# Products without a reader on TensorE in its waits, and GpSimd's last additions moved behind the logits

## The reference, cut to what matters

```python
x = x + 0.5 * quant_ffn(ln(x))          # int8 rounding of tokens and weight, 256 -> 256
x = x + linear_attention(ln(x))         # elu(q) + 1, elu(k) + 1, no softmax
x = x + 0.5 * quant_ffn(ln(x))
x = x + 0.5 * routed_mlp(ln(x))
x = x + softmax_attention(ln(x))
x = x + 0.5 * routed_mlp(ln(x))

def routed_mlp(x):                      # per batch
    logits = x @ Wr + br
    weights, idx = top_k(logits, 128)   # 128 of 1024 tokens, in order of their index
    tokens = sort(idx)
    out = gelu(x[tokens] @ W1 + b1) @ W2 + b2
    return x.at[tokens].add(softmax(weights) * out)
```

## Time and profile before

| | us |
|---|---|
| median of three runs | 3504.67 |
| lowest and highest | 3502.99, 3505.31 |
| the profiled execution, its own time | 3506.28 |
| its span, first to last instruction | 3504.5 |

### The profile page before, as it was taken

How to read it: one execution, slowest core, us unless ns; L and a number is a source line. 1 busy time by engine, 2 the same in 40 slices (tenths; PEclk the granted TensorE clock), 3 DMA queues, 4 the chain that set the end, 5 groups by cost and what they waited for, 6 DMA issues and landing times.

```text
span 3504.5 us, 52704 instructions
## 1 busy us (share of the span) xinstructions
PE 3339.6 (95%) x19398; PEld 2861.0 (82%) x19398; DVE 2666.2 (76%) x4957; ACT 2044.9 (58%) x3908; POOL 1057.1 (30%) x1274
## 2 busy tenths in 40 slices
PE   3898999989999999999999999999999999999995
PEld 2777878868888888888888888888888888888884
DVE  5788796767876787876788677886778767876776
ACT  3676767646556556556565556555555565556552
POOL 3786656632222112122121221212212131213112
PEclk8999999999999999999999999999999999999997
DMA  2221212110001000001000001000000010001000
GB/s 83 70 85 50 66 55 70 58 37 13 13 19 29 15 13 13 15 23 28 13 14 13 25 19 43 13 13 25 25 14 14 13 34 28 16 19 29 26 19 20
DMA packets 98525, 104.21 MB, mean 30 GB/s; under 512 B 10336, under 2 KB 88800, under 8 KB 98144
## 3 DMA queue, kind: packets, MB, share of 16 engines
q1 hardware_dynamic: 98272, 100.85, 9.7%
HBM read 87.18 MB, written 13.63 MB: 29 GB/s over the span
## 4 chain that ended last, share of the span: by engine, by line
PE 70%; DVE 6%; ACT 3%; DMA 0%; issue 0%; POOL 0%; DVEq 0%; SPq 0%; ACTq 0%; POOLq 0%
PE at_ps_job L1927 12%; PE at_ps_job L35 7%; PE at_ps_job L37 7%; PE at_ps_job L36 6%; PE at_ps_o L35 6%; PE at_ps_o L37 6%; PE at_ps_o L36 6%; PE at_ps_s L35 6%; PE at_ps_s L36 6%; PE at_ps_s L37 6%; DVE at_neg_max L1854 1%; ACT x_resident L1678 1%; DVE at_probT_lo L1721 1%; PE at_ps_job L646 1%; DVE at_oT_lo L1752 0%; DVE ch_r L97 0%
## 5 line engine op out<-in xcount | busy, mean ns | idle before, releaser
L1637 ACT ACTIVATE at_probT_hi<-at_ps_job 128x512 fp32r<-128x512 f32 x1024 | 611.4, 598 | 889.9 <-PE at_ps_job L1927 887.2
L1721 DVE TENSOR_TENSOR at_probT_lo<-at_ps_job,at_probT_hi 128x512 fp32r<-128x512 f32 x1024 | 702.8, 686 | 275.5 <-ACT at_probT_hi L1637 265.1
L1678 ACT ACTIVATE x_resident<-at_ps_s,at_neg_max 128x1024 f32<-128x1024 f32 x512 | 570.7, 1115 | 151.6 <-DVE at_neg_max L1854 146.5
L1854 DVE TENSOR_REDUCE at_neg_max<-at_ps_s 128x1 f32<-128x1024 f32 x512 | 622.2, 1215 | 5.3
L1927 PE MATMUL at_ps_job<-ident,x_resident 128*128 128x128 f32 x4096 | 613.7, 272 | 5.0 <-DVE at_probT_lo L1721 3.4
L1927 PEld LDWEIGHTS at_ps_job<-ident,x_resident 128*128 128x128 f32 x4096 | 495.9, 140 | 97.7 <-issue 7.3
L35 PE MATMUL at_ps_o<-at_probT_hi,at_v_lo 128*128 128x512 f32 x1024 | 446.3, 436 | 8.9 <-DVE at_oT_lo L1752 7.8
L1613 POOL TENSOR_TENSOR at_w_hi<-at_w_raw,ch_cols 128x256 fp32r<-128x256 f32 x192 | 117.6, 613 | 1107.1 <-PE at_ps_job L37 1086.3
L35 PE MATMUL at_ps_s<-at_k_hi,at_q_lo 128*128 128x512 f32 x1024 | 445.1, 435 | 0.0
L37 PE MATMUL at_ps_o<-at_probT_lo,at_v_hi 128*128 128x512 f32 x1024 | 404.6, 395 | 0.0
L36 PE MATMUL at_ps_s<-at_k_hi,at_q_hi 128*128 128x512 f32 x1024 | 402.0, 393 | 0.0
(11 more groups left out here) (347 smaller groups left out, 7480.8 us busy)
## 6 DMA issues: line engine op xcount, KB each, us to landing
at_w_raw<-attn_w SPq DMA_DIRECT2D x256, 128.0 KB, 2.3
at_w_raw<-mlp_w SPq DMA_DIRECT2D x112, 128.0 KB, 2.3
li_wo_hi<-li_wo_kept SPq DMA_DIRECT2D x24, 256.0 KB, 2.7
li_wo_lo<-li_wo_kept SPq DMA_DIRECT2D x24, 256.0 KB, 3.0
li_wq_hi<-li_wq_kept SPq DMA_DIRECT2D x48, 128.0 KB, 2.3
li_wq_lo<-li_wq_kept SPq DMA_DIRECT2D x48, 128.0 KB, 2.8
x_resident<-x SPq DMA_DIRECT2D x4, 1024.0 KB, 13.1
out<-x_resident SPq DMA_DIRECT2D x4, 1024.0 KB, 4.9
```

What stands on the lines that cost most here:

```text
L1637: nc.scalar.activation(ph[:, i // TC, 4 * half:4 * half + 4, (i % TC) * P:(i % TC + 1) * P], c.turned_bank(2 * TB * u + 2 * i + half), ACT ...
L1678: nc.scalar.activation(prob[:, slot % 2, :], ps_s[slot % 2][:], ACT.Exp, bias=nmax[:, slot:slot + 1], accum_out=rsum[:, u % 2, slot:slot + ...
L1721: nc.vector.tensor_tensor(pl[at], c.turned_bank(2 * TB * u + 2 * i + half), ph[at].bitcast(F32), ALU.subtract).then_inc(s_pl, 1)
L1854: nc.vector.tensor_reduce(nmax[:, slot:slot + 1], ps_s[slot % 2][:], AX.X, ALU.max, negate=True).then_inc(s_max, 1)
```

## The change

Six places change. A helper issues `count` products with the bfloat16 identity as the stationary operand, each with 512 bfloat16 columns; each starts and stops its own accumulation and no engine reads its result before the bank is written anew. It is called

- in the first layer, after the turns of the weight's scales, 34 times, into the last bank of `ps_y`;
- in the linear attention at the head of PE's stream, 22 times, into bank 7;
- in the last layer, into `ps_job[0]`, 20 times before `rows_out(1)` and behind the waits ahead of it, 24 times before `gather(0)`, 20 times before `gather(1)`.

And GpSimd waits for `f_l` to reach 2, which is when all eight tiles have their logits, before its eight additions in the last layer.

```diff
+def idle_products(nc, sh, bank, moving, count):
+    for _ in range(count):
+        nc.tensor.matmul(bank, sh.identb[:], moving, start=True, stop=True)
...
             last.then_inc(s_wt, 1)
+            idle_products(nc, sh, ps_y[-1][:].rearrange("p a d -> p (a d)"), wq[:].rearrange("p a d -> p (a d)"), 34)
             pe.wait_ge(s_v, 10)
...
+            idle_products(nc, sh, ps[:, 7, :], sh.wqT[:].rearrange("p k d -> p (k d)"), 22)
             pe.wait_ge(s_ones, 2 * TB)
             for t in range(BEGIN, plan.end):
...
             ln_rstd(nc, pool, sh, ln, 1, 4, 4)
+            pool.wait_ge(f_l, 2)
             for j in range(TB):
                 pool.wait_ge(f_half, j + 1)
...
             pe.wait_ge(c.took, max(by_act.values()))
+            idle_products(nc, sh, ps_job[0][:], sh.wqT[:].rearrange("p k d -> p (k d)"), 20)
             rows_out(1)
+            idle_products(nc, sh, ps_job[0][:], sh.wqT[:].rearrange("p k d -> p (k d)"), 24)
             gather(0)
+            idle_products(nc, sh, ps_job[0][:], sh.wqT[:].rearrange("p k d -> p (k d)"), 20)
             gather(1)
```

## The result

The changed kernel takes **3496.46 us** (median of 19 executions, 3495.21 to 3499.31); the kernel before takes 3504.97 us (19 executions, 3502.99 to 3506.37). The ratio is 0.9978, with an interval of 0.9971 to 0.9984: 8.5 us by the medians, 0.22 to 0.24% faster. That is past the 0.2% line of the prediction, but the interval (0.16 to 0.29%) reaches to both sides of it. The profiled execution after took 3497.92 us with a span of 3495.9, so the two spans differ by 8.6 us, like the medians.

A forecast was written before the change was run, and what follows sets the result against it. PE was taken to bound the long middle and VectorE to set the end. The terms -1.6 - 3.6 + 0.5 - 0.5 + 0.5 - 1.9 = -6.6 us, from the median 3504.67, gave 3498.1 us, range 3494.4 to 3502.2.

The forecast's parts named there:

- (1): First layer, 34 products after the weight's turns: costed at nothing, hidden by GpSimd's run of additions.
- (2): Start of the linear attention, 22 products: second low part sooner by 0.9 to 2.6 us, taken as -1.6.
- (3): Last layer, GpSimd's additions held behind the logits: VectorE's normalisations -1.5 and dot products -2.1, together -3.6 us.
- Rival C: Last layer: GpSimd's additions slow VectorE's comparisons, +3.5 on the forecast, 3501.6 us; chance 0.08.
- (4): Last layer, 20 products before the second row of logits: +0.5 us late (0 to 2.1), four turns faster, -0.5.
- (5): Last layer, 24 and 20 products around the first gather: +0.5 us late (0 to 1.6), second gather faster, -1.9.
- (6): Hidden layer's second half, at low clock before: whether shifted work meets that fall unreadable, taken as 0 (0 to -1.4).
- A: Whole kernel: the clock holds everywhere, no late filler, hidden layer 1.4 us shorter: -10.0, 3494.7 us; chance 0.20.
- B: Start: nothing gained, the clock falls in pauses or lower clock later eats the advance: -5.0, 3499.7 us; chance 0.22.
- D: Start and last layer: fillers outlast their gaps, all at the low clock: +7.9, 3512.6 us; chance 0.04.
- E: Whole kernel: fillers run, clock moves at other times, only GpSimd's wait counts: -3.6 + 1.0 late, 3502.1 us; chance 0.06.

The follow-up runs named there:

- experiment 5: The change without the 34 products of the first layer: 3499.18 us, ratio 0.9984 to the kernel before.
- experiment 8: The change with 7 more products behind the linear attention's first turns and 20 at the head of the attention's PE stream: 3498.14 us, ratio 0.9978.
- experiment 2: The change without GpSimd's wait, all products kept: 3499.89 us, ratio 0.9988 to the kernel before.
- experiment 4: The kernel before with the 34 and the 22 products at the start alone: 3503.61 us, ratio 1.0.
- experiment 6: The change without the 22 products of the linear attention: 3498.64 us, ratio 0.9983 to the kernel before.
- experiment 1: The kernel before with GpSimd's wait added and no products: 3502.01 us, ratio 0.9996.
- experiment 10: The change with GpSimd's additions held back further, behind the eighth comparison instruction: 3502.37 us, ratio 0.9993 to the kernel before.
- experiment 9: The change with products of 254 columns in six waits of PE for VectorE in the linear attention: 3493.90 us, ratio 0.9970 to the kernel before.
- experiment 12: Experiment 9 without the 34 products of the first layer, with a seventh place and more products: 3493.51 us, ratio 0.9968 to the kernel before.
- experiment 11: The change without the 20 products before the second row and the 24 before the first gather: 3500.29 us, ratio 0.9989 to the kernel before.
- experiment 3: The kernel before with only the last layer's 20, 24 and 20 products, without the wait: 3502.05 us, ratio 0.9991.
- experiment 7: The change with 40, 48 and 40 products in the last layer, twice as many: 3506.51 us, ratio 1.0005 to the kernel before.

## Why the prediction was right, and where it was not

The forecast was 3498.1 with a range of 3494.4 to 3502.2; 3496.46 lies in it. The direction had 0.42 for faster by over 0.2% and 0.54 for within it; it came out at 0.22 to 0.24%, so near the line that another set of runs could fall on the other side, and which side it fell on is luck. The mechanism is the forecast's, but three sizes were off, in both directions: the start won less, no filler of weight was late, and the hidden layer won 1.2 that was put at nothing. By the steps:

**(1) 34 products, 0: right** by the stages, and so was the cover: GpSimd's additions, which stand where they stood with them and without (experiment 5). The medians can't confirm it to better than some 3 us.

**(2) 22 products, -1.6: -1.1** at the second low part and -1.5 at the last statistics. The mechanism was the one foreseen, a fall of the clock in the middle of the products. But its size is not one number. Over the ten profiled executions that have the 22 (the 7 more of experiment 8 among them) the second low part stood between 49.57 and 51.98, and over before and the three without them between 51.70 and 52.18; the means, experiment 8 left out, are 50.9 and 52.0. The two values in which the clock held without the 7, 49.57 and 49.65, were those whose 22 products took longest (7.39 and 7.82 us, 6.3 to 7.2 in the others); in experiment 2 PE's first work behind them came late, at 43.87, and the clock was low from the second product on. That the lead is carried to the end was assumed. It is shown as far as the first query: from the second low part to there all these executions took 44.7 to 45.1 us. Behind it the stretch to the attention scatters between 621.2 and 625.7 us, and whether 1.1 us is left at the end on the median stays open (experiments 4 and 6). The Trainium skill, "TensorE: Matmul & The Clock Gate", section "What's actually happening", says that one kernel's count of slow products at its start differs from run to run; the traces agree (of the twelve K and V products none is slow in experiment 4, whose start is that of the change, and seven are in after).

**(3) The wait, -3.6: -3.7** (-3.65 alone, in experiment 1). Rival C's price, 3.5 for slowed comparisons, is 0 (and 3.5 was loosely worked out: 6.2 us of additions at the paces 0.87 and 0.34 give 3.8): their lengths agree to 0.01 us beside the additions and without. The contention that was left out since it was 1.7 us clear of the one-hots is real, and dearer than its 1.5: 2.75 - 0.88 = 1.9 for the four, 0.7 more for the two sums before them (experiment 10). In the change the additions end at 3463.57, 2.4 us ahead of the one-hots. The Trainium skill, "SBUF — State Buffer", section "Who interferes with whom", has it so on both sides, and the traces agree: comparisons untouched, plain tensor_scalar from SBUF and sums of two SBUF inputs held up.

**(4) 20 before the second row, +0.5 late and -0.5: 0 and -0.5.** The 20 were to begin 0.05 us ahead of the last statistics (3452.9) and take 7.4 us, 13 of them low; they began 0.03 us behind them and took 6.6 (3451.50 to 3458.12). With 0.427 for a low one (512 columns at the low pace of 45 to 49 us) and 0.216 for a high one, that is eleven low. They ended as the logits arrived: the turns start 0.14 us behind the end of the logits' last step (3457.98), as with PE at rest (0.15, experiment 1). It was close: in experiments 6, 9, 10 and 12 they start 0.26 to 0.36 behind it, so the 20 were 0.1 to 0.2 late there.

**(5) 24 and 20, +0.5 late and -1.9: 0 and -1.7.** The feared fall in front of the first gather did come (3.44 us), and yet the 20 behind it were all high (19 records in 4.26 us) and ended with the second one-hots. The prediction's bound of +1.6 is close to what experiment 11 shows when nothing has raised the clock before: +1.4.

**(6) The hidden layer, 0: -1.2**, the largest miss. The step that failed is "whether the shifted work meets that fall is not to be read; I take 0": its end of the range, -1.4, was the nearer one. Over all fourteen kernels: the stage took 4.15 in after and in experiments 2, 3, 5, 6, 8, 9 and 12, and 5.3 to 5.4 in before, 1, 4, 7, 10 and 11. The eight at 4.15 are those in which fillers stood ahead of the second gather and it started in time, 16.26 to 16.28 us behind the first comparison. In before, 1 and 4 no fillers stood ahead of it; in 7, 10 and 11 they did, but it started late, at 21.01, 19.21 and 17.67. So the same fillers can leave the hidden layer at either clock; what exactly decides was not separated, since no run changed the time between the fillers and the hidden layer alone.

The sum: -6.6 + 0.1 for (2), - 0.1 for (3), - 0.5 for (4), - 0.5 + 0.2 for (5) and - 1.2 for (6) makes -8.6. (For (2) this takes the -1.5 at the last statistics, of which 0.4 came somewhere between 51 and 3451 us and may be scatter.)

**The rivals.** A, the clock holds everywhere: it fell at 46.3 and before the first gather, so no, but its -1.4 for the hidden layer and its lack of late fillers came. B: the start gave something in the profiles up to the first query, though by the times of experiments 4 and 6 it cannot be told from nothing; B's second form, a lead lost again later, is left open. C fell with experiments 1 and 10. D is a real mechanism: full with twice the fillers (experiment 7), in part where the clock is low before the last 20 (experiment 11). E: without the wait the products alone are worth 3.45 us of the last layer (experiment 3), so no.

## What to carry to other kernels

Products that nobody reads pay where PE's wait ends in its own work on the critical path, and only if they end before that work is due: count them at the low pace for the first half and the high one after (here nine of the 34 and eleven of the 20 before the second row were low), and see in the trace that the wait's end does not move. Where another engine sets the time behind the wait, as GpSimd did twice here, they buy nothing. And elementwise work on GpSimd was best placed beside VectorE's comparisons, which read PSUM, not beside plain operations that read SBUF only: here the same eight additions cost 3.7 us in one place, nothing in the second and 2.6 in the third.

## What was not expected of the hardware

- Products without a reader move the clock as real ones do: with 36 of 254 columns in a pause of 4.5 us the work behind it ran at 0.12 pace instead of 0.21.
- Behind six of the seven long pauses for `li_f` in the linear attention the products run at half pace for a while, in a stretch whose mean clock of 0.97 looks full. With seven waits filled the low level held for 4 us there, not 32, and the kernel is some 3 us faster on the median, about as much as all fillers of the last layer won (3.45).
- The clock's changes fall at other times from one execution to the next: with the same instructions up to there the second low part stood at 49.65 in experiment 4 and at 51.98 in experiment 2, 2.3 us apart, twice what the change wins there. A single profile can't price such an edit.
- A VectorE sum of four elements went from 0.16 to 0.65 us beside GpSimd. One of GpSimd's additions takes 0.69 (5.51 us for eight), so it looks as if the small sum waits for a whole one whatever its own size; that is our reading, not shown.
